# K and V of all pairs in the first phase, by way of DRAM, in a cross-attention and FFN kernel

## The reference

```python
x = x + xattn(layernorm(x), ctx, ctx, Wq, Wk, Wv, Wo)
x = x + ffn(layernorm(x), w_gate, s_wgate, w_up, s_wup, w_down, s_wdown, inv_gate, inv_up, inv_inter)

def xattn(query, key, value, Wq, Wk, Wv, Wo):
    q = heads(query @ Wq, 32); k = heads(key @ Wk, 8); v = heads(value @ Wv, 8)
    k, v = repeat(k, 4), repeat(v, 4)
    probs = softmax(q @ k.T * 32 ** -0.5)
    return merge(probs @ v) @ Wo

def ffn(x, ...):
    qg, sg = dynamic_quant(bfloat16(x), inv_gate); qu, su = dynamic_quant(bfloat16(x), inv_up)
    inter = silu(qg @ w_gate.T * sg * s_wgate) * (qu @ w_up.T * su * s_wup)
    qi, si = dynamic_quant(bfloat16(clip(inter, -10, 10)), inv_inter)
    return qi @ w_down.T * si * s_wdown
```

## Time and profile before

| | |
|---|---|
| median of three executions | 784.54 us |
| all three | 783.48, 785.12, 784.54 us |
| span of the profiled execution, first to last instruction | 782.1 us |
| its own time | not given apart; it lies with the three above, 1.3 to 3.0 us over the span |
| busy PE, DVE, ACT, POOL | 694.3, 570.1, 271.4, 216.2 us |
| mean granted clock of TensorE | 0.959 |
| moved by DMA | 71.24 MB, 91 GB/s in the mean |

### The profile page before, as it was taken

How to read it: one execution, slowest core, us unless ns; L and a number is a source line. 1 busy time by engine, 2 the same in 40 slices (tenths; PEclk the granted TensorE clock), 3 DMA queues, 4 the chain that set the end, 5 groups by cost and what they waited for, 6 DMA issues and landing times.

```text
span 782.1 us, 13916 instructions
## 1 busy us (share of the span) xinstructions
PE 694.3 (89%) x5072; PEld 426.2 (54%) x5072; DVE 570.1 (73%) x820; ACT 271.4 (35%) x417; POOL 216.2 (28%) x170
## 2 busy tenths in 40 slices
PE   3866889999999999999999999999999999758843
PEld 2753475457755675467655775557646764333321
DVE  4744564699758975898669975897679966886663
ACT  4542344143414343233315342333314340433230
POOL 3020100442142503242244204241234213232331
PEclk9995799999999999999999999999999999989985
DMA  7465468411232232222141223213232003112000
GB/s 295 145 219 180 128 194 258 115 35 52 88 100 70 52 109 78 88 57 79 47 121 50 60 85 100 67 51 108 70 95 54 31 20 112 46 52 78 1 27 27
DMA packets 36256, 71.24 MB, mean 91 GB/s; under 512 B 8816, under 2 KB 17008, under 8 KB 36208
## 3 DMA queue, kind: packets, MB, share of 16 engines
q1 hardware_dynamic: 33920, 62.42, 25.9%
q0 software_dynamic: 2304, 8.39, 2.8%
HBM read 44.43 MB, written 8.52 MB: 68 GB/s over the span
## 4 chain that ended last, share of the span: by engine, by line
PE 54%; DVE 16%; issue 13%; POOL 6%; SPq 4%; DMA 3%; ACT 3%; DVEq 0%; POOLq 0%; ACTq 0%
PE bank L459 20%; PE bank L531 13%; PE bank L567 4%; POOL xs L1462 3%; PE bank L421 3%; PE bank_s L478 3%; PE bank_o L508 2%; PE bank L589 2%; POOL rstd L1447 2%; DVE neg_max L1160 2%; PE bank_d L512 2%; DVE amax L1197 2%; PE bank_s L496 2%; SPq L317 2%; SPq L297 2%
## 5 line engine op out<-in xcount | busy, mean ns | idle before, releaser
L459 PE MATMUL bank<-act_t_hi,wq_hi 128*128 128x256 f16 x512 | 140.6, 275 | 2.5 <-DVE act_t_lo L1123 2.1
L459 PE MATMUL bank<-act_t_hi,wq_lo 128*128 128x256 f16 x512 | 140.4, 274 | 0.0
L459 PE MATMUL bank<-act_t_lo,wq_hi 128*128 128x256 f16 x512 | 140.3, 274 | 0.0
L1160 DVE TENSOR_REDUCE neg_max<-bank_s 128x4 f16<-128x512 f32 x128 | 82.4, 684 | 46.5 <-PE bank_s L478 46.3
L1169 DVE RECIPROCAL o_norm<-bank_d 128x512 f32<-128x512 f32 x32 | 107.3, 3353 | 12.2 <-PE bank_d L512 11.1
L1467 POOL TENSOR_TENSOR o_t_lo<-o_norm,o_t_hi 128x512 f16<-128x512 f32 x32 | 40.0, 1250 | 220.2 <-ACT o_t_hi L912 220.2
L898 ACT ACTIVATE probs<-bank_s 128x512 f32<-128x512 f32 x128 | 71.6, 596 | 78.6 <-PE bank_s L496 48.1
L531 PE MATMUL bank<-wo_hi,o_t_hi 128*128 128x512 f16 x256 | 97.4, 380 | 0.8 <-POOL o_t_lo L1467 0.8
L531 PE MATMUL bank<-wo_hi,o_t_lo 128*128 128x512 f16 x256 | 97.1, 379 | 0.0
L531 PE MATMUL bank<-wo_lo,o_t_hi 128*128 128x512 f16 x256 | 97.0, 379 | 0.0
L1462 POOL TENSOR_TENSOR xs<-xb,inv_up 128x1024 f32<-128x1024 bf16 x16 | 34.3, 2141 | 110.8 <-ACT code_g L947 110.8
(11 more groups left out here) (107 smaller groups left out, 1292.8 us busy)
## 6 DMA issues: line engine op xcount, KB each, us to landing
inp<-in_ctx_t SPq DMA_DIRECT2D x16, 512.0 KB, 4.8
inp<-in_x SPq DMA_DIRECT2D x16, 512.0 KB, 3.4
q_stack<-q_st_hi SPq DMA_DIRECT2D x128, 64.0 KB, 2.0
x<-in_x SPq DMA_DIRECT2D x16, 512.0 KB, 4.8
out<-x POOLq DMA_DIRECT2D x16, 512.0 KB, 3.0
q_stack<-q_st_lo SPq DMA_DIRECT2D x64, 64.0 KB, 2.0
x<-in_wo SPq DMA_DIRECT2D x6, 512.0 KB, 3.8
x<-in_wq SPq DMA_DIRECT2D x4, 512.0 KB, 6.5
```

Of the source, the lines that this page charges most:

```text
L459: ins = nc.tensor.matmul(bank[:, :, jj, :], wq_sb[a][:, 2 * item + jj, kc, :], act_t[m][:, kc, :, :], start=(kc == 0 and (a, m) == PARTS[0 ...
L1160: nc.vector.tensor_reduce(neg_max[:, c:c + REP], bank_s[g % 2][:, :].rearrange("p (j n) -> p j n", j=REP), AX_X, ALU.max, negate=True).the ...
```

## The change

K and V of all eight pairs are computed in `start()`, in two other banks (`bank3`, which the first output projection uses later). ctx has three fp32 slots in the tiles of the gate, up and down weights, and its split parts have four slots in the tiles of the output projection's weights; those weights are loaded and split after the last K and V (`weights_hi` waits at piece 12 and at piece 20). K and V go to DRAM, one spill a pair, and come back one batch at a time. Q of a pair goes to DRAM in two DMAs and to its stack in three for each batch. `load_ctx` and POOL's `ctx` are gone from the steady part, and the lists of all five engines are in another order.

```diff
+        k_dram = nc.dram_tensor("k_dram", (2, NB, P, KVD), F16, kind="Internal").ap()
+        q_dram = nc.dram_tensor("q_dram", (2, PAIRS, P, 2, NT * REP * P), F16, kind="Internal").ap()
+        v_dram = nc.dram_tensor("v_dram", (NB, P, KVD), F32, kind="Internal").ap()
...
+        ctx_slots = [flat(t).bitcast(F32) for t in (wgu_sb[0], wgu_sb[1], wd_sb)]
+        act_slots = [flat(wo_sb[h])[:, i * 4 * D:(i + 1) * 4 * D] for h in ("hi", "lo") for i in range(2)]
...
+            def spill_k(p):
+                sp.wait_ge(kv_free, NKV1 * p + KV["k1"] + 1)
+                for h in range(2):
+                    sp.dma_start(k_dram[h, 2 * p:2 * p + 2].rearrange("b p n -> p b n"),
+                                 k_st[("hi", "lo")[h]][:, :, :, :].rearrange("p b t n -> p b (t n)")).then_inc(k_spilled, 16)
...
             def fill_k(p, b):
                 r = 2 * p + b
-                sp.wait_ge(s1_free, N1 * p + S1["k1"] + 1)
...
-                for g in range(4):
-                    rows = slice(HD * g, HD * g + HD)
-                    for i, h in enumerate(("hi", "hi", "lo")):
-                        sp.dma_start(k_stack[HD * i:HD * i + HD, g, :, :], k_st[h][rows, b, :, :]).then_inc(k_stacked, 16)
+                for i, h in enumerate((0, 0, 1)):
+                    sp.dma_start(k_stack[HD * i:HD * i + HD, :, :, :].rearrange("p g t n -> p g (t n)"),
+                                 k_dram[h, r].rearrange("(g d) n -> d g n", g=4)).then_inc(k_stacked, 16)
...
+            def spill_q(p):
+                sp.wait_ge(s1_free, N1 * p + S1["q3"] + 1)
+                passed(sp, p)
+                for h in range(2):
+                    sp.dma_start(q_dram[h, p], q_st[("hi", "lo")[h]][:, :, :, :].rearrange("p b t n -> p b (t n)")).then_inc(q_spilled, 16)
...
             def fill_q(p, b):
                 r = 2 * p + b
+                sp.wait_ge(q_spilled, 32 * p + 32)
...
+                for i, h in enumerate((0, 1, 0)):
+                    sp.dma_start(q_stack[HD * i:HD * i + HD, :, :, :].rearrange("p g t n -> p g (t n)"),
+                                 q_dram[h, p, :, b].rearrange("(g d) n -> d g n", g=4)).then_inc(q_stacked, 16)
...
             def weights_hi(n):
                 act.wait_ge(w_loaded[slot_of[n]], 16 * uses[n])
+                if n == W_O:
+                    act.wait_ge(kv_full, NKV1 * PAIRS)
+                if n == W_GATE:
+                    act.wait_ge(ctx_split, 2 * PAIRS)
...
             def steady(nxt, cur, prv):
...
-                k(nxt, 0, 0)
                 s(cur, 0, 6)
...
-                v(nxt, 0)
-                v(nxt, 1)
```

More of the change, by code:

```diff
@@ L141, in build @@
         w_lo = sem("w_lo")
-        ctx_loaded = [sem(f"ctx_loaded{b}") for b in range(2)]
+        ctx_loaded = [sem(f"ctx_loaded{i}") for i in range(6)]
         x_loaded = [sem(f"x_loaded{b}") for b in range(2)]
@@ L384, in finish @@
                 fill_k(last, 0)
+                spill_q(last)
                 load_res(last - 1, 0)
@@ new lines, in start @@
+                v(3, 1)
+                q(0, 1, 1)
+                q(0, 1, 2)
+                q(0, 1, 3)
+                k(4, 0)
+                q(0, 2, 0)
+                q(0, 2, 1)
+                k(4, 1)
+                q(0, 2, 2)
+                v(4, 0)
+                q(0, 2, 3)
+                v(4, 1)
+                k(5, 0)
+                q(0, 3, 0)
+                q(0, 3, 1)
+                q(0, 3, 2)
+                q(0, 3, 3)
+                k(5, 1)
+                v(5, 0)
@@ L959, in start @@
                 ctx_hi_(0, 0)
+                weights_hi(0)
                 ctx_hi_(0, 1)
-                for n in range(0, 5):
-                    weights_hi(n)
-                hi(0, "k0")
-                hi(0, "k1")
+                weights_hi(1)
+                weights_hi(2)
+                weights_hi(3)
+                k_hi_(0, 0)
+                ctx_hi_(1, 0)
+                hi(0, "x00")
+                k_hi_(0, 1)
+                ctx_hi_(1, 1)
+                weights_hi(4)
+                k_hi_(1, 0)
@@ L1277, in start @@
                 lo(0, "x11")
-                for n in range(6, 11):
-                    weights_lo(n)
-                lo(0, "q0")
+                v(1, 1)
+                k_lo(2, 0)
+                k_lo(2, 1)
+                weights_lo(6)
+                v(2, 0)
+                weights_lo(7)
+                ln1_stats(1, 0)
+                v(2, 1)
+                weights_lo(8)
+                k_lo(3, 0)
+                lo(0, "q0")
+                ln1_stats(1, 1)
+                k_lo(3, 1)
@@ L1394, in finish @@
                 quant(last - 1, 1, 0)
+                max_(last, 1, 0)
                 dn(last - 1, 0, 0)
+                max_(last, 1, 1)
                 dn(last - 1, 0, 1)
+                max_(last, 1, 2)
+                max_(last, 1, 3)
+                max_(last, 1, 4)
+                max_(last, 1, 5)
+                max_(last, 1, 6)
+                max_(last, 1, 7)
                 quant(last - 1, 1, 1)
-                for n in range(0, 8):
-                    max_(last, 1, n)
                 gscale(last - 1, 1, 0)
```

951 lines of the change are left out of this document (562 added, 389 removed).

## The result

The changed kernel is **slower**: 803.78 us, median of four runs (799.78 to 809.25), against 784.01 (782.72 to 785.12, four runs) for the kernel before; the ratio is 1.0242, 95% interval 1.0179 to 1.0306. I had predicted 767.3 us, with a range of 749 to 785.

What follows compares the result with a forecast made beforehand. A steady turn was taken as bound by TensorE, the start as not, with 35.4 us idle. Start +38.0, six turns -49.2, finish -6.0 sum to -17.2: 764.9 us span, 767.3 us with 2.4 around it, range 749 to 785.

Steps and rivals of the forecast that it cites:

- The stacks: Steady turn: row 0's Q goes to DRAM and back in 8.0 to 9.0 us, within 10.8 us of cover.
- Row 1's "1.3 us": Steady turn: wait booked at the stacks for row 1, fill 5.6 to 6.6 us against 5.9 of cover.
- The sign of a gap: Whole kernel: waits counted at their length; the clock term only a gain in the start, 7 us.
- K and V: Steady turns: 10.5 us of matmuls leave each, 83.4 to 72.9 of work; turn 85.2 to 77.0, six turns -49.2.
- my bound was 74.7: Steady turn: lower bound with no new waits, -63 us over six turns.
- The start: Start takes 63.0 us more work, fills idle time and regains clock: 173.4 us, +38.0.
- the 7 us come back: Start: added matmuls fill gaps, so the clock rises and work shrinks by 7 us; otherwise the start would be 180.
- the rival: Start bound by loads and conversions: 38 MB at 204 GB/s is 186 us, total 785 us, no change; 8%.
- The lower bound of 166: Start: its shortest time, with no idle but the head's and the clock up, rounded up.
- The finish: Finish: row 1's scores start earlier since the stack fills sooner; -6 us, between nothing and -9.
- The trip through DRAM becomes the wait: Rival, steady turns: Q's spill and fill outlast their cover, 7.8 us of waits a turn, 806 us; 8%.
- the 2.4 us that I put around the span: Whole kernel: time outside the profiled span, added to 764.9 us to give 767.3.

Runs made afterwards that it cites:

- e14: e10 with an idle gap of TensorE, made by two GpSimd subtractions without a DMA, ahead of row 0's first score in six turns and the finish: 794.19 us.
- e6: The changed kernel with row 0's first two scores of a steady turn three output-projection groups later in TensorE's order: 789.81 us.
- e3: The changed kernel with Q's stack filled only once, later stores and fills of Q left out, so the result is wrong: 762.6 us.
- e12: The changed kernel once more, with no edit: 804.27 us.
- e11: The kernel before with only K and V moved to the start (its new order included), turns and finish in old order, Q copied direct: 843.12 us.
- e10: e9 with the finish of TensorE, VectorE, ACT and POOL in the order of the kernel before: 762.45 us.
- e8: The changed kernel with both rows' Q copied straight from its tile to the stack by twelve 64 KB copies, no store to DRAM: 846.51 us.
- e5: The changed kernel with Q's trip through DRAM kept but begun earlier, in halves, with a second pair of stacks in dead weight tiles: 774.61 us.
- e9: e5 with the first turn's loads (x of pair 2, row 0's residual) issued in the start, ahead of Q's half trip of pair 1: 767.58 us.
- e13: e10 with matmuls of no use filling TensorE's gaps in the last 50 us: 763.37 us.

## Why the prediction was wrong, point by point

**The stacks** are the step that failed. "8.0 to 9.0 us" for row 0's trip against "10.8 together" of cover. The cover was right: from 342.3 to 352.8, 10.5 us. The trip took 12.6. Its terms: SP reaches the stores 1.1 us late, since three fills of K stand ahead of them (forecast: nothing); stores 4.2 to the next issue, as forecast (1.2 + 3.0); the fill, "3 x 0.6 + 2.0 to 3.0", took 7.2 (347.63 to 354.87) in place of 3.8 to 4.8. I priced a 256 KB copy by its neighbours, 64 KB in 2.0 and a store of 512 KB in 3.0. But three of them follow one another, of 2 KB pieces into 32 partitions each, and they land 4.6, 5.5 and 6.1 us after their issues. The stretches of the store and of the fill in the changed kernel:

```profile
343.40:347.40 4.00, 4.00 (x25) 1.48 (x16) 3.28 (x2) 0.00 (x0) 3.34 (x4) 1.00 0.75 290
347.60:354.60 7.00, 5.20 (x25) 2.13 (x22) 5.31 (x12) 0.62 (x1) 1.70 (x3) 1.00 0.95 232
```

In the fill's stretch the DMA engines are busy 0.95 of the time at 232 GB/s, the residual's load and an output store included; the median landing is 5.5 us after the issue, the whole span's 4.7. The neighbours are the smaller part of it: row 1's three fills in the finish, issued from 700.10 right behind K's and with no other DMA issued until they have landed at 706.03, take 5.9 us. By the fit of the Trainium skill, "DMA: Bandwidth & Descriptors", section "Anatomy of one DMA", which the page gives for single copies issued by GpSimd (SP issues these), the three fills would be an estimated 3.8 us and the two stores 4.4. The trace is near it for the stores (4.0) and not for the fills (7.0 and 5.9). Row 1's "1.3 us" was 0.6 to 1.1 in the loop turns.

**The sign of a gap.** I counted waits at their length. e14 shows 4.7 us for 3.0; e6 gives 2.8 to 3.0 a turn for a wait of 2.0 to 2.5. Over the kernel Q's way is worth 41 us (803.8 to 762.6 in e3). The waits for both stacks in the profile, K's included, are 4.8 in the start, 7.8 in the first turn, some 3.0 in each of five, and 7.1 in the finish, 34 in all; its span is 48.9 us above that of e3 (e12: 31.5 of waits, 43.6 above). The rest, 12 to 15 us, is the clock's, as far as e14's rows carry over. I had given the clock a term, but only as a gain in the start. By the Trainium skill, "TensorE: Matmul & The Clock Gate", Part 1, the array is throttled by default and sustained activity releases it: e14's rows agree (0.43 us apart behind the gap, 0.215 again from 430.45), and I should have applied the rule to each wait that I booked.

**K and V.** "72.9 us of work" in a turn: 72.1 to 72.2 at full clock. That the turn can be 74.2 holds (my bound was 74.7). That it follows from taking the work out does not: e11 takes out the same work and stays at 85.2. The reasoning "bound by TensorE, idle 1.8, so 10.5 less work is 10.5 less time" was false; the new order of all engines makes the gain (74.2 in e10), and it in turn needs Q's tile to be free early (83.5 to 85.7 in the turns behind the first of e8), which the same trip through DRAM provides.

**The start**, 173.4, came out only where Q's trip is left out (172.7 in e3). The changed kernel has 178.4 and 183.0, with waits of 2.4 to 2.9 and 1.9 to 2.1 us for the two stacks, and a clock of 0.77 between 150 and 172 us (0.88 in e12) where e3 has 1.00. But these waits are not all: e5, e9, e10 and e13 hide the trip and still start with 177.7 to 180.4 (clock 0.79 in the same stretch of e10), so 4 to 7 us over the forecast stay open. That "the 7 us come back" holds in e3 (busy 149.8), not in the changed kernel (153 to 158). On the loads: "five more pairs of ctx" are six, 6.3 MB and a sum of 39 MB; the start moved 37.9. They were no bound of the size that the rival has, since e3's start moves the same bytes but row 1's fill in 172.7 us. The lower bound of 166 is 168.4 by its own terms.

**The finish.** "-6 us, since row 1's scores come earlier": wrong even without the trip. In e9 the first of them starts 37.2 us into the finish, ten earlier than before (47.1), but the second 45.6, since the FFN's items stand between (TensorE stands 5.0 us for ACT's `inter` there), and the transpose of the maxima comes at 52.3 against 53.8; the finish is 140.9. So earlier scores brought the maxima 1.5 us and the finish nothing. The new order there costs 5.4 us (e9 to e10); the trip and its clock cost 5.0 to 7.9 (the changed kernel's 145.9 and 148.8 against e9's 140.9). Which item of the new order costs the 5.4 wasn't separated.

**The rivals.** "The trip through DRAM becomes the wait", 806 us at 8%, is what happened, but that its 806 lies so near 803.8 is luck. Its price for a turn was too high (7.8 us of waits; 2.7 to 3.2 measured) and it left out the first turn, where the trip meets the loads (7.2 us), the finish and the clock. Two terms of the trip, SP's late arrival and the length of the fill, made it: the chance was far too low for a step whose trip and cover stood within 2 us of one another.

**The sum.** e9, the changed kernel with the trip hidden and the first loads early, takes 767.58 us, and I had forecast 767.3. That is luck too: its start is 5.4 us over the forecast, its turns are 2.9 under it each, its finish 11.4 over. And the 2.4 us that I put around the span are 1.65 in the changed kernel (809.25 against 807.6).

## What to carry to other kernels

Before work is taken out of a full engine, ask what it covers: strike it out alone and time it, or follow the chain of the other engines through the same turn; here a busy share of 98% did not mean that this engine alone set the time. Price a two-hop transfer (one that goes out to DRAM and comes back) by issue, each landing with what else is in flight, and what stands ahead in its queue; if it comes within two us of its cover, hide it in full, here with a second stack in tiles that are dead and half of the transfer sent a turn earlier. And count a gap of TensorE in a full stretch at more than its length: here 4.7 us for 3.0 in a turn, and 31.7 for 19.1 over the kernel (e14).

## What the runs showed of the hardware

Behind a gap of 3.0 us made by GpSimd, in a stretch at full clock, TensorE's matmuls start 0.43 us apart for 3.4 us, then 0.215 again (e14). Behind gaps of the changed kernel that a DMA made the lower level is seen too, but not always as long: about 3.5 us behind 2.1, 2.9 behind the first turn's 7.2, 5.9 behind the 3.2 in the finish. Behind row 1's gap of 0.8 us in the loop turn the matmuls keep their full pace. Three copies of 256 KB from DRAM into 32 partitions each, 2 KB a piece, take 7.0 us from the first issue to the last landing, and 5.9 where no other DMA is issued until they have landed; two of 512 KB from 128 partitions to DRAM take 4.0. Whether the pieces or the partitions make the fills so long was not separated. In the first turn the second store lands after 7.3 us, where it takes 3.4 in the loop turn: two loads of x and K's three fills, issued ahead of it, were then still in flight.
